# A state-space mixing stage: the next batch's first scan, two layer norms and their places in VectorE's program

## What is computed

```
x = x + tanh(g_xattn[0]) * mamba(ctx, z=layernorm(x))
x = x + tanh(g_ffn[0]) * ffn(layernorm(x))
...
def mamba(ctx, z):                      # per batch; 512 channels e, 512 positions l, 16 states n
    u     = silu(conv4(in_proj(ctx)) + conv_b)
    dt_low, Bm, Cm = split(x_proj(u))
    delta = softplus(dt_proj(dt_low) + dt_b)
    state[e,n] = state[e,n] * exp(delta[e,l]*A[e,n]) + delta[e,l]*u[e,l]*Bm[n,l]     # over l
    y[e,l]     = sum_n state[e,n]*Cm[n,l] + D[e]*u[e,l]
    return (y * silu(z)).T
def ffn(x):
    h = silu(x @ w_gate) * (x @ w_up)
    return top2_of_4(h) @ w_down
```

## Time and profile before

| | |
|---|---|
| median of three runs | 4199.0 us |
| profiled execution | 4200.4 us |
| its span | 4198.9 us |
| TensorE busy | 3734.7 us (89%) |
| VectorE busy | 3069.5 us (73%) |
| ScalarE busy | 1683.8 us (40%) |
| first stage, to VectorE's last output | 0 to 868 us |
| first feed-forward batch's last down products begin | 1038.8 us |

### The profile page before, as it was taken

One profiled execution on the slowest core, in us unless ns is written; L12 is line 12 of the kernel. 1 busy time (PEld: TensorE's weight loads), 2 busy tenths in 40 slices (PEclk: granted clock), 3 DMA queues, 4 the chain that ended last, 5 costly groups with the idle time before them and its releaser, 6 DMA issues.

```text
span 4198.9 us, 41456 instructions
## 1 busy us (share of the span) xinstructions
PE 3734.7 (89%) x12733; PEld 1940.3 (46%) x12786; DVE 3069.5 (73%) x4986; ACT 1683.8 (40%) x2649; POOL 669.8 (16%) x647
## 2 busy tenths in 40 slices
PE   5988888989999998999984999899999999998656
PEld 3555655644444444444432444454554554553222
DVE  6787778768889788888898554575574673774887
ACT  4767676632333322433331011254352452551322
POOL 1433333433333110333210000000000000000000
PEclk8999999999999999999996999899999999999887
DMA  3323232424242322444432000221121110110000
GB/s 106 118 91 114 91 115 85 170 109 151 89 154 85 137 81 91 157 154 153 160 113 88 1 0 0 81 71 53 36 71 36 54 64 25 63 56 33 10 10 20
DMA packets 92131, 346.25 MB, mean 82 GB/s; under 512 B 12160, under 2 KB 20480, under 8 KB 78496
## 3 DMA queue, kind: packets, MB, share of 16 engines
q1 hardware_dynamic: 61888, 226.90, 15.1%
q0 software_dynamic: 30048, 116.94, 8.0%
HBM read 281.40 MB, written 62.39 MB: 82 GB/s over the span
## 4 chain that ended last, share of the span: by engine, by line
PE 55%; DVE 25%; issue 10%; ACT 6%; DMA 3%; POOL 0%; DVEq 0%; ACTq 0%; SPq 0%; POOLq 0%
PE ps L994 36%; PE ps L1339 5%; PE ps L1068 4%; PE ps L1329 3%; PE ps L1216 2%; DVE room L1491 2%; PE ps L1164 2%; DVE room L1495 2%; PE ps L1061 1%; DVE room L1499 1%; DMA room<-bc_scratch 1%; DVE stat L1453 1%; DVE room L1504 1%; DVE stat L1955 1%; DVE room L1960 1%
## 5 line engine op out<-in xcount | busy, mean ns | idle before, releaser
L994 PE MATMUL ps<-room 128*128 128x512 bf16 (+1 forms) x2873 | 955.7, 490 | 99.3 <-ACT room L942 49.0
L994 PE MATMUL ps<-lnT,room 128*128 128x512 f32 x2240 | 990.5, 598 | 22.6 <-DVE room L1685 8.1
L590 POOL TENSOR_TENSOR idle<-idle 128x1 f32<-128x1 f32 x288 | 477.8, 1659 | 1502.2 <-ACT room L795 553.3
L994 PEld LDWEIGHTS ps<-lnT,room 128*128 128x128 f32 x2240 | 427.2, 192 | 570.3 <-issue 534.7
L994 PEld LDWEIGHTS ps<-room 128*128 128x128 bf16 (+1 forms) x2912 | 401.2, 141 | 623.8 <-issue 329.0
L1164 PE MATMUL ps<-room 128*128 128x512 f32 x864 | 379.0, 596 | 8.5 <-DVE room L1637 8.5
L669 ACT ACTIVATE room<-room,small 128x511 f32<-128x511 f32 x256 | 163.6, 709 | 367.1 <-DVE room L1495 354.8
L994 PE MATMUL ps<-down_rows,room 128*128 128x256 f32 x1024 | 250.2, 400 | 47.5 <-ACT room L789 45.2
L1552 DVE TENSOR_TENSOR_SCAN room<-room 128x2048 f32<-128x2048 f32 x64 | 283.2, 4424 | 6.2
L1495 DVE TENSOR_TENSOR_SCAN room<-room 128x2048 f32<-128x2048 f32 x64 | 283.4, 4428 | 5.4
L1919 DVE TENSOR_REDUCE stat<-ps 128x1 f32<-128x512 f32 x256 | 177.1, 692 | 131.8 <-PE ps L994 131.8
(11 more groups left out here) (217 smaller groups left out, 4912.3 us busy)
## 6 DMA issues: line engine op xcount, KB each, us to landing
kv_stash<-room POOLq DMA_DIRECT2D x128, 256.0 KB, 2.7
room<-in_ffn SPq DMA_DIRECT2D x16, 2048.0 KB, 10.9
room<-bc_scratch POOLq DMA_DIRECT2D x128, 256.0 KB, 3.6
room<-kv_stash SPq DMA_DIRECT2D x64, 512.0 KB, 3.5
room<-stash POOLq DMA_DIRECT2D x24, 1024.0 KB, 9.5
room<-in_ffn SPq DMA_DIRECT2D x20, 1024.0 KB, 5.0
room<-in_ffn SPq DMA_DIRECT2D x12, 1536.0 KB, 7.9
room<-bc_scratch SPq DMA_DIRECT2D x64, 256.0 KB, 3.7
```

The lines of the kernel that those rows point to most:

```text
L590: nc.gpsimd.tensor_tensor(idle[:, :], idle[:, :], idle[:, :], ALU.add).then_inc(zeros_added, 1)
L994: last = nc.tensor.matmul(out, lhsT, rhs, start=(i == 0), stop=(i == len(parts) - 1))
```

## The change

In the first stage, VectorE's product and scan of a state become a function `state_of`. State 0 of batch 0 is done ahead of the loop; state 0 of batch b + 1 is done at the end of batch b, behind `m_du` and ahead of the output. The gate's layer norm of a batch is made in that batch behind state 9, no longer at the end of the batch before. In the last batch VectorE makes the feed-forward's layer norm of batch 0 ahead of the last output; ScalarE and TensorE drop their wait for the first stage's last `x_done` at the head of the feed-forward. SP loads the row of state 0 ahead of the loop and at the end of each batch but the last, and `m_kctx` behind the row of state 1.

```diff
--- before.py
+++ after.py
@@ -426,16 +426,17 @@
 
                 store_bc(0, 0, first_tiles("x", 0)[0])
 
+                sp.wait_ge(bc_stored[0], 16)
+                sp.dma_start(m_bc[0], bc_row(0, 0, 0)).then_inc(bc_loaded[0], 16)
+
                 def body(b, last):
                     tile = batch_tiles(b, last)
                     for n in range(DS):
-                        row = bc_row(0, b, n)
-                        if n == 0:
-                            sp.wait_ge(bc_stored[0], b * 16 + 16)
-
-                        sp.wait_ge(scan_done, b * DS + max(n - (NBC - 1), 0))
-                        sp.dma_start(m_bc[n % NBC], row).then_inc(bc_loaded[n % NBC], 16)
-                        if n == 0:
+                        if n:
+                            row = bc_row(0, b, n)
+                            sp.wait_ge(scan_done, b * DS + (n - 1))
+                            sp.dma_start(m_bc[n % NBC], row).then_inc(bc_loaded[n % NBC], 16)
+                        if n == 1:
                             sp.wait_ge(tile_filled, tile("h", 0, 0)[0])
                             sp.dma_start(m_kctx, ctx_d[bass.ds(b * P, P), :]).then_inc(kctx_loaded, 16)
                         if n == 2 and not last:
@@ -449,6 +450,11 @@
                             sp.wait_ge(stash_ready, b + 1)
                             for place, buf in zip(places, (m_nd2, m_u2, m_zT)):
                                 sp.dma_start(place, buf).then_inc(stash_stored, 16)
+                    if not last:
+
+                        row = bc_row(0, b + 1, 0)
+                        sp.wait_ge(scan_done, b * DS + (DS - 1))
+                        sp.dma_start(m_bc[0], row).then_inc(bc_loaded[0], 16)
                 batches(sp, body)
                 load_ctx(0, tile_filled, batch_tiles(B - 1, True)("in", 1, NE - 1)[0] + 1)
                 sp.wait_ge(stash_stored, B * 48)
@@ -818,7 +824,8 @@
 
             def ffn(stage, s):
                 T = TILES[s]
-                act.wait_ge(x_done, B * stage)
+                if s:
+                    act.wait_ge(x_done, B * stage)
                 take_lnT(stage, 0)
 
                 def body(b, last):
@@ -1124,7 +1131,8 @@
 
             def ffn(stage, s):
                 T = TILES[s]
-                pe.wait_ge(x_done, B * stage)
+                if s:
+                    pe.wait_ge(x_done, B * stage)
                 transpose_ln(stage, 0)
 
                 def body(b, last):
@@ -1463,8 +1471,6 @@
                     dve.wait_ge(tr_done, (b + B * LNT[stage]) * NK)
                 elif stage:
                     dve.wait_ge(g_z_ready, b)
-                elif not (isinstance(b, int) and b == 0):
-                    dve.wait_ge(tile_filled, batch_tiles(b - 1, False)("z", NT - 1)[0] + 1)
                 for t in range(NT):
                     last = v.tensor_scalar(ln3[:, t, :], x_tile(b, t), mv[:, 2 * t:2 * t + 1], rs[:, t:t + 1],
                                            ALU.subtract, ALU.mult)
@@ -1538,19 +1544,24 @@
                     dve.wait_ge(sp_corrected, f + 1)
                     v.tensor_tensor(m_delta, m_nd, m_w, ALU.add).then_inc(delta_ready, 1)
 
+                def state_of(b, n):
+
+                    Bn = m_bc[n % NBC].unsqueeze(1).broadcast_to([P, NE, S])
+                    h = m_h[n % 2]
+                    dve.wait_ge(bc_loaded[n % NBC], b * (DS // NBC * 16) + (n // NBC + 1) * 16)
+                    link(v.tensor_tensor(t3(h, NE), t3(m_du, NE), Bn, ALU.mult))
+                    dve.wait_ge(dA_ready, b * DS + (n + 1))
+                    v.tensor_tensor_scan(h, m_dA[n % 2], h, 0.0, ALU.mult, ALU.add).then_inc(scan_done, 1)
+
                 def body(b, last):
                     front_b, front_a = 2 * b + 1, 2 * b + 2
                     tile = batch_tiles(b, last)
-                    for n in range(DS):
-                        Bn = m_bc[n % NBC].unsqueeze(1).broadcast_to([P, NE, S])
-                        h = m_h[n % 2]
-                        dve.wait_ge(bc_loaded[n % NBC], b * (DS // NBC * 16) + (n // NBC + 1) * 16)
+                    for n in range(1, DS):
                         if n >= 2:
                             dve.wait_ge(tile_filled, tile("h", n - 2, NT - 1)[0] + 1)
-                        link(v.tensor_tensor(t3(h, NE), t3(m_du, NE), Bn, ALU.mult))
-                        dve.wait_ge(dA_ready, b * DS + (n + 1))
-                        v.tensor_tensor_scan(h, m_dA[n % 2], h, 0.0, ALU.mult, ALU.add).then_inc(scan_done, 1)
-
+                        if n == 14 and not last:
+                            dve.wait_ge(bc_stored[0], b * 16 + 32)
+                        state_of(b, n)
                         if n == 2:
                             dve.wait_ge(stash_stored, b * 48)
                             convolve(front_b, 1, tile)
@@ -1559,6 +1570,8 @@
                             convolve(front_a, 0, tile)
                         if n == 7:
                             softplus(front_b, 1)
+                        if n == 9:
+                            layernorm(stage, b)
                         if n == 10:
                             dve.wait_ge(sp_ln, front_b + 1)
                             dve.wait_ge(sp_corrected, front_b + 1)
@@ -1574,7 +1587,11 @@
                     if not last:
                         dve.wait_ge(delta_ready, b + 2)
                         link(v.tensor_tensor(m_du, m_delta, m_u, ALU.mult))
-                        layernorm(stage, b + 1)
+                        dve.wait_ge(tile_filled, tile("h", DS - 2, NT - 1)[0] + 1)
+                        state_of(b + 1, 0)
+                    else:
+                        dve.wait_ge(tile_filled, tile("z", NT - 1)[0] + 1)
+                        layernorm(stage + 1, 0)
 
                     dve.wait_ge(nsum_done, b * DS + DS)
                     dve.wait_ge(tile_taken, tile("z", NT - 1)[0] + 1)
@@ -1592,15 +1609,15 @@
                     ins = v.tensor_scalar(t3(m_diag, NE)[:, e, :], ident[:, :], const(("dd", 0))[:, e:e + 1], None, ALU.mult)
                 ins.then_inc(diag_ready, 1)
                 convolve(0, 0, first_tiles)
-                dve.wait_ge(x_loaded, 16 * B)
-                layernorm(stage, 0)
                 softplus(0, 0)
                 take_next(0, 0)
                 dve.wait_ge(delta_ready, 1)
                 link(v.tensor_tensor(m_du, m_delta, m_u, ALU.mult))
+                state_of(0, 0)
+                dve.wait_ge(x_loaded, 16 * B)
                 front = 3 + 1
-                n = DS + front + 1
-                chain.batches_peeled(n + front + 1 + LN_LINKS, n, body)
+                n = DS + front + 1 + LN_LINKS
+                chain.batches_peeled(n + front + 1, n - 1 + LN_LINKS, body)
 
             def gate_mamba(stage):
 
@@ -1661,7 +1678,8 @@
                     v.tensor_scalar(f_ds, rows_sb[s], tg(stage), None, ALU.mult)
 
                 v.memset(t3(s_dA, NE)[:, :, 0:1], 0.0)
-                layernorm(stage, 0)
+                if s:
+                    layernorm(stage, 0)
 
                 def body(b, last):
                     t = 0
```

## The result

The changed kernel takes 4171.4 us (median of four runs, 4170.65 to 4171.95), the kernel before beside it 4201.7 us (4193.92 to 4204.99): a ratio of 0.993, 95% interval 0.9913 to 0.9948. The forecast was 4168.6 us in a range of 4157 to 4184. The profiled execution took 4171.58 us for a span of 4170.0, at a mean granted clock of 0.952. The span is 28.9 us shorter than before; the prediction's sum was 30.4.

The account below looks back on a forecast made before the run. The order written for VectorE was taken to stall TensorE and ScalarE at first-stage batch ends, and TensorE at the stage's end. Savings of 19.4 + 11.0 = 30.4 us put the median at 4168.6 us, range 4157 to 4184.

Parts of the forecast that it names:

- What falls away at a repeat is ScalarE's wait, 4.96 and 5.01, and 9.40 at the exit: First-stage batch ends: ScalarE's wait for scan 0 vanishes, 4.96 us into batch 1, 5.01 into 2, 9.40 into 3.
- TensorE's head products follow with the same gain: Start of batches 1 to 3: TensorE's head products start earlier by what ScalarE gains, if its own 16 transposes start in time.
- slower: the clock: Rival, 0.03: new short waits repeatedly halve TensorE's clock in the first feed-forward batches, 3.6 us a fall; twelve falls give 4212 us.
- part 1: Three first-stage batch ends: the next batch's state 0 product and scan go ahead of the output, saving 19.4 us.
- The turn of ScalarE's loop costs 4.7, and TensorE's no more than that: First-stage batch ends: ScalarE's 4.70 us delay stays at both repeats; TensorE's unseen loop turn was taken as 4.7 too.
- TensorE's turn is long: Rival, 0.12: TensorE's loop turn costs 11 us, so both repeats gain nothing; 20.4 us saved, 4178.6 us.
- A turn is free: Rival, 0.04: the 4.70 us is no part of the turn, so each batch end gains 9.4; 4159.8 us.
- Part 2 costs nothing: Gate's layer norm behind state 9: hidden in VectorE's waits for ScalarE's logarithm; priced at nothing, bounds 0 and 4.1 us.
- It makes room for part 1: Moving the gate's layer norm from the batch end frees VectorE for the next batch's state 0, 6.7 us of work.
- Part 3 gives 11.0: First stage's end: feed-forward layer norm before the last output, two waits dropped; 11.0 us saved, bounds 7.5 and 15.9.
- The sum: Whole kernel: 19.4 us at batch ends plus 11.0 at the stage's end, 30.4 saved.

Follow-up runs that it names:

- e1: Kernel before plus only the feed-forward's first layer norm ahead of the first stage's last output, its two waits dropped; 4188.25 us, ratio 0.9976.
- the repeat: The changed kernel run again, unchanged, in the second session; 4176.10 us, ratio 0.9951 to the kernel before.
- e2: Changed kernel with the feed-forward's first layer norm behind the last output as before, and ScalarE and TensorE waiting for it; 4184.09 us, ratio 0.9967.
- e3: Changed kernel plus six useless products on TensorE behind the small transposes at the end of batches 0 to 2; 4172.69 us, ratio 0.9941.
- e11: Changed kernel with ScalarE's loop of the first stage written out for all four batches; 4167.65 us, ratio 0.9929 to the kernel before.
- e4: Changed kernel with ScalarE's exponentials of the next batch's state 2 ahead of the small copies and its loop turn; 4167.83 us, ratio 0.9928.
- e6: Changed kernel with the gate's layer norm behind state 9 done twice; 4178.11 us, ratio 0.9959 to the kernel before.
- e5: Changed kernel with the gate's layer norm back at the batch's end, behind the next batch's scan and ahead of the output; 4177.85 us, ratio 0.9958.
- e8: Changed kernel with GpSimd's feed-forward load of delta issued after the last sum of states, and `y` behind B and C; 4168.65 us, ratio 0.9939.

## Why the prediction came out as it did

*What falls away at a repeat is ScalarE's wait, 4.96 and 5.01, and 9.40 at the exit.* Right at the place it names: the head products start 5.25, 5.51 and 9.60 us earlier on the batch before.

*TensorE's head products follow with the same gain.* They start with it, and this is the step that failed: the prediction gave the lower clock behind the new pauses no price at a batch's start. At the first repeat the head products take 2.6 us longer than before, at the second another 0.8 goes, and inside batches 2 and 3 4.5 us in all. Inside batch 2 the pauses are as before, but three groups are slow instead of one. In batch 3 it is three instead of two, and pauses move: those ahead of states 12 and 13 (0.97 and 1.45) go, and the one ahead of state 14, for the load of its weight, grows from 0.69 to 2.46. This part is more than the luck of one trace: inside the batches 7 groups are slow in both traces with the old batch ends (before and e1), and 8 to 10 in all eleven others. Why is open. Against that, the starts gained 1.0 more than forecast and the exit's head products another 1.0. The sum for part 1 was 19.4; what arrived at the last output, counted from the end of batch 0, is 15.2 - 1.8 = 13.4 (12.8 - 2.6 = 10.2 in the repeat, 10.4 in e2). e3 is the test: with the pause filled the same repeats give 5.2 and 6.8. The rival *slower: the clock* had the mechanism, but looked for it in the feed-forward, where VectorE does cover the one fall at 901, and not in the first stage, where a slow group delays all that follows.

*The turn of ScalarE's loop costs 4.7, and TensorE's no more than that.* Right: 4.55 and 4.53 after, gone in e11 and moved, not shortened, in e4. TensorE's own turn shows no pause, so *TensorE's turn is long* is out. *A turn is free* is out by the same rows. In "Runtime: NRT & Kernel Launch", Instruction fetch mechanics, the Trainium skill has a taken branch wait where its target isn't loaded; that fits a delay which the exit doesn't have. No run here shows the fetch itself.

*Part 2 costs nothing.* Right, by e6, for batches 0 to 2; in batch 3 TensorE has no wait for a scan in the changed kernel either. *It makes room for part 1.* Wrong: the earlier trace rows show VectorE idle for 7.14 us behind the layer norm and 6.7 us of work come in, so there was room without it, as e5 shows. Both numbers were in the prediction and weren't set against each other.

*Part 3 gives 11.0.* 10.4 to 10.5 in every kernel that has it with the loads as they were. Delta was put 5.2 us behind its issue and landed in 5.1, the first state product was to start 9.9 us earlier against the last sum and starts 9.2 earlier (865.52), the wait of 1.14 went. What the sum missed is a term of ScalarE's: it has one table load between delta's landing and the first gate activation, and the trace has two (859.05 and 862.91, 1.28 each), as the trace before had. So that activation stands 16.1 us behind the last sum and not 14.9, and the chain over delta binds by 0.7 us, not the one over B's row that the prediction ended with (B's row lands 8.7 us behind 856.14).

*The sum.* 28.9 against 30.4 in the profiled execution is closer than its terms were: part 1 fell short by 6.0 and part 3 by 0.6, 1.8 were there at the end of batch 0, which nobody had counted and the change can't be credited with, and the untouched later stages gave 3.2. That the sum fits is in part luck: 5.0 of the 28.9 are none of the prediction's. In the repeat those stages lost 0.8, and the time was 4176.1. The saving of this change is 20 to 30 us by these two sessions; the range held both.

## What to carry to other kernels

Before you price a removed wait, look at what runs on the waiting engine right behind it: if TensorE waits a few us, the next group can pay for the clock. Here the transposes paid 1.4 us for it (3.40 against 1.96) and the head products 2.6, so small work is the better thing to have in that place; no run tried to reorder them. A delay marked "issue" at a long loop's end was worth as much as a wait of the same length, and on ScalarE it went when the loop was written out. Ask of each part of a change whether the other parts need it: an idle time and a length of work, read from the same rows, answer that ahead of any run.

## What the runs showed of the hardware

A pause between groups of products can halve TensorE's clock, and can leave it. The 13 traces have 832 groups of 16 head products in the first stage, which take 3.6 to 3.7 us at full clock. Over 5 us are:

| idle time before the group, us | groups | over 5 us |
|---|---|---|
| none | 499 | 0 |
| 0.67 to 1.47 | 62 | 0 |
| 1.74 to 2.46 | 195 | 70 |
| 2.54 to 3.14 | 49 | 40 |
| 4.08 to 7.60 | 27 | 27 |

The same pause goes both ways: behind 2.39 us once 5.41 and once 3.72, behind 2.90 once 3.72 and once 5.41 in the same run of e11, behind the exit's 3.14 once each 5.38, 6.51 and 6.60 (the repeat, e8, e2) and three times 3.69 (the changed kernel, e5, e6). Which of the short ones are hit differs from one execution of the same kernel to the next. In the two traces of the changed kernel the end of the first stage differs by 2.4 us.

The end of ScalarE's loop costs 4.5 to 4.7 us where it goes round, 0.16 where it is left, and nothing once written out. TensorE's, with a longer body (some 750 products a batch against some 220 instructions of ScalarE's), shows no pause at all, nor does VectorE's (the output's second operation ends at 261.77, the next product starts at 261.69); why they differ was not tried.

Stages that a change doesn't touch shift against the kernel before by up to 3 us at a time and sum up to several us, in both directions (+3.2 in the changed kernel, +5.9 in e8, -5.2 in e3, from the norm to the end). A difference of under 6 us between two single traces of this kernel says nothing unless it is read at the place of the edit.
